# SyncE's first loads in a four-block transformer kernel: x of batches 2 and 3 wait for W_k, W_o moves behind the middle parts of batch 0

## Chip, cores and metric

One core of a Trainium2 chip runs the whole kernel in one launch. The metric is the device time in microseconds (us), the median of several executions; smaller is better.

## What is computed

Four residual blocks, each followed by a layer norm, over x of 4 batches x 256 tokens x 256 features in fp32: causal attention with 16 heads of 16, a gated feed-forward block of width 704, a second attention with biases, and a second feed-forward block of width 1024 with ternary weights.

```
x = layernorm(x + attention0(x, w_project, w_out))
x = layernorm(x + ffn0(x, gate_w, up_w, down_w, gate_s, up_s, down_s))
x = layernorm(x + attention1(x, Wq, bq, Wk, bk, Wv, bv, Wo, bo))
x = layernorm(x + ffn1(x, ternary(W_up), ternary(W_gate), ternary(W_down)))

attention: q, k, v = projections of x
           softmax(causal(q @ k.T / 4)) @ v, then @ w_out.T
```

## The kernel before

Each batch goes through every block on its own. The order of the work of each of the five engines is written out by hand, as a text of steps `STEP:lbi`, where l is the layer, b the batch and i the part (`QK:000` is the q projection of layer 0, batch 0, `QK:001` its k projection, `QK:000-1` both). An engine walks its list in order and waits on semaphores; nothing overtakes on one engine.

Precision comes from splitting. A weight or an activation is kept as a high part and the rest (`wa_hi` and `wa_lo`, `xT_hi` and `xT_lo`), and a product takes three matmuls (lines 566 to 568). q and k are cut into three bf16 parts, high (`QK`), middle (`MID` on SyncE, `SPLIT` on the computing engines) and low (`LO`). SyncE stacks the parts into `q_stack` and `k_stack` with a DMA for each place that a part has in the stack: three for a high part, two for a middle one, one for a low one, each 128 KB. TensorE's first score product `S:000` waits for all twelve of batch 0.

The beginning is what the change touches:

- SyncE (line 481 on) issues the four quarters of layer 0's attention weights, each 256 KB (`load_a0(sp, n)`, line 472: W_q, W_k, W_v, W_o for n = 0 to 3) and x of batches 1 to 3 (`load_x`, line 476), then the list `SYNC_STEPS`: `LOAD:003` is W_o, `LOAD:001` three small loads of biases (lines 520 to 522), then the stacks (line 538).
- ScalarE loads the transposed x of batch 0 itself (line 789). Step `PREPA` n (line 795) copies quarter n into `wa_hi` and waits for that quarter's load; its list reads `... SPLIT:010 PREPA:002 SPLIT:011 PREPA:003 QK:020-1 SPLIT:020-1 QK:030 ...`.
- VectorE takes the rest of each quarter (`PREPA`, line 966) and the rest of q and k (`QK`, line 994): `... QK:011 QK:020 PREPA:002 QK:021 PREPA:003 S:000-2 QK:030 S:003-7 ...`. `S` (line 1009) takes the maxima of a score tile out of PSUM and sets its banks free for TensorE, `MB` (line 1032) joins them, `MX` (line 1041) makes the low part of the maxima, which SyncE sends into the stack (line 545) ahead of the second score product `ST`.
- TensorE: `QK:000 XI:010 QK:001 QK:010 XI:020 XI:030 QK:011 QK:020-1 QK:030 S:000-2 V:000 S:003-7 ...`. `XI` (line 592) transposes x of a batch and waits for its load.

```
if step == "PREPA":
    c = slice(i * D, (i + 1) * D)
    act.wait_ge(a0_in[i], 16)
    nc.scalar.activation(wa_hi[:, :, c], raw_a[:, :, c], ACT.Copy).then_inc(wa0_hi, 1)
```

W_o itself is first multiplied in step `O:000`, some 40 us later; the space `raw` in which the quarters land is taken again by the load `RAW:000`, which waits for all four `PREPA` of VectorE.

Of the kernel before, what the change touches and what calls it, by code (L numbers as in the profile page):

```python
# [147 lines left out]
    HI:120 LN:310 HI:121-3 HI:130-3 LN:320 LT:130-1  # L148
"""
SYNC_STEPS = """  # L150
    LOAD:003 LOAD:001 QK:000-1 MID:000-1 LO:000-1 QK:010-1 LO:010-1 MID:010-1 RAW:000 LOAD:000 LO:020 RAW:001 LO:021
    MX:000 ML:000 MID:020-1 QK:020-1 RAW:002 MX:010 RAW:003 QK:030-1 ML:010 RAW:004-5 MID:030 LO:030-1 MID:031
    LOAD:002 RAW:006 MX:020 ML:020 RAW:007-10 MX:030 ML:030 RAW:0011-25 QK:100 RAW:0026-27 MID:100-1 RAW:0028 QK:101
    LO:100-1 RAW:0029-30 QK:110 MID:110-1 QK:111 LO:110-1 QK:120 MX:100 ML:100 LO:120-1 QK:121 MID:120-1 MX:110
# [26 lines left out]
def program(nc, x_nat, x_tr, a0, f0gu, f0dn, gs, us, ds_row, a1, bqk, bv, bo_row, f1, out):  # L181
# [13 lines left out]
    def nth(step, l=0, b=0, i=0):  # L195
        return count[(step, l, b, i)]
# [12 lines left out]
    def nb_of(l, b):  # L209

        return NB * l + b

    def users(l, b):

        return batches[max(0, nb_of(l, b) - SLOTS):max(0, nb_of(l, b) - SLOTS + 1)]
# [14 lines left out]
    with ctx:  # L230
# [3 lines left out]
        def sem(name):  # L234
            return ctx.enter_context(nc.semaphore(name))
# [73 lines left out]
        a0_in = [sem(f"a0_in{n}") for n in range(4)]  # L309
# [131 lines left out]
        def raw_of(piece, width):  # L441

            r = PIECES.index(piece)
            first = 1024 * (r % 2) if r < PREP0 else 512 * ((r - PREP0) % 2)
            return raw[:, first:first + width]
# [6 lines left out]
        def raw_used(piece):  # L452

            kind, n = piece
            return {"PREP0": (w_lo, n + 1) if n < 4 else (dn_scaled, n - 3), "PREP1": (w_lo, PREP0 + n + 1),
                    "AB": (abs_done, n + 1), "TERN": (tern_done, n + 1)}[kind]
# [6 lines left out]
        def columns_of(n):  # L463

            m, r = n // 4, n % 4
            r = (0, 2, 1, 3)[r] if m < 2 else r
            return m, slice(512 * r, 512 * (r + 1))

        def load_a0(queue, n):

            c = slice(n * D, (n + 1) * D)
            queue.dma_start(raw_a[:, :, c], a0[:, :, c]).then_inc(a0_in[n], 16)

        def load_x(queue, b):

            queue.dma_start(x[:, TT * b:TT * (b + 1), :], x_nat[:, TT * b:TT * (b + 1), :]).then_inc(x_in[b], 16)
# [4 lines left out]
        @block.sync  # L481
        def _(sp):

            load_a0(sp, 0)
            load_a0(sp, 1)
            load_x(sp, 1)
            load_a0(sp, 2)
            load_x(sp, 2)
            load_x(sp, 3)

            for step, l, b, i in sp_order:

                if step == "RAW":
                    kind, n = PIECES[i]
                    if i < 2:
                        sp.wait_ge(wa0_lo, 4)
                    elif i < PREP0 or i >= PREP0 + 2:
                        sp.wait_ge(*raw_used(PIECES[i - 2]))
                    else:

                        sp.wait_ge(*raw_used(PIECES[PREP0 - 1]))
                    landed = raw_in[i % 2]
                    if kind == "PREP0" and n < 4:
                        sp.dma_start(raw_of(PIECES[i], W0), f0gu[:, n // 2, (n % 2) * W0:(n % 2 + 1) * W0]).then_inc(landed, 16)
                    elif kind == "PREP0":
                        sp.dma_start(raw_of(PIECES[i], 512), f0dn[:, (n - 4) * 512:(n - 3) * 512]).then_inc(landed, 16)
                    elif kind == "PREP1":
                        sp.dma_start(raw_of(PIECES[i], 512).rearrange("p (k n) -> p k n", k=KT),
                                     a1[:, :, n * D:(n + 1) * D]).then_inc(landed, 16)
                    else:  # L510
                        m, c = columns_of(n)
                        sp.dma_start(raw_of(PIECES[i], 512), f1[:, m, c]).then_inc(landed, 16)
                if step == "LOAD":

                    if i == 0:
                        sp.dma_start(gs_c[:, :], gs).then_inc(scales_in, 16)
                        sp.dma_start(us_c[:, :], us).then_inc(scales_in, 16)
                        sp.dma_start(ds_b[:, :], ds_row.partition_broadcast(P)).then_inc(scales_in, 16)
                    if i == 1:
                        sp.dma_start(qk_bias[:, :], bqk).then_inc(bias_in, 16)  # L520
                        sp.dma_start(bv_c[:, :], bv).then_inc(bias_in, 16)
                        sp.dma_start(bo_b[:, :], bo_row.partition_broadcast(P)).then_inc(bias_in, 16)
                    if i == 2:
                        load_x(sp, 0)
                    if i == 3:
                        load_a0(sp, 3)
                if step in ("QK", "MID", "LO"):
                    n = nb_of(l, b) % SLOTS
                    stack, stacked, blocks = ((q_stack[n], q_stacked[n], Q_BLOCKS),
                                              (k_stack[n], k_stacked[n], K_BLOCKS))[i]  # L530
                    part, done = {"QK": (0, qk_hi), "MID": (1, qk_mid), "LO": (2, qk_lo)}[step]
                    if users(l, b):

                        sp.wait_ge(st_mm, nth("ST", *users(l, b)[0], NS - 1))
                    sp.wait_ge(done, nth("QK", l, b, i))
                    for r in range(len(blocks)):
                        if blocks[r] == part:
                            sp.dma_start(stack[r:KP:len(blocks), :, :].rearrange("p h t -> p (h t)"),
                                         part_of[nb_of(l, b) % 2][i][part][:, :]).then_inc(stacked[part], 16)
                if step in ("MX", "ML"):  # L540

                    n = nth("MX", l, b, i)
                    row, done, part = (KP, maxT_hi_done, maxT_hi) if step == "MX" else (KP + 1, maxT_done, maxT_lo)
                    sp.wait_ge(done, n)
                    sp.dma_start(q_stack[nb_of(l, b) % SLOTS][row:row + 1, HH * i:HH * (i + 1), :].rearrange("p h t -> p (h t)"),
                                 part[n % 2][:, :]).then_inc(max_rows[n % 2], 16)
                if step == "LN" and l == 3:
                    sp.wait_ge(ln_done, nth("LN", l, b))
                    sp.dma_start(out[:, TT * b:TT * (b + 1), :], x[:, TT * b:TT * (b + 1), :]).then_inc(stored, 16)
                if step == "LT":  # L550
                    sp.wait_ge(tail_done, i + 1)
                    sp.dma_start(out[:, TT * b + i:TT * b + i + 1, :], x[:, TT * b + i:TT * b + i + 1, :]).then_inc(stored, 16)
            sp.wait_ge(stored, 16 * (NB - 1 + TT))
# [234 lines left out]
        def _(act):  # L788
            act.dma_start(xT_raw[:, :, :], x_tr).then_inc(xT_in, 16)
            for step, l, b, i in act_order:  # L790
# [57 lines left out]
                if step == "ST":  # L848
                    n = nth("ST", l, b, i)
                    if n == 1:  # L850
                        act.wait_ge(xT_done, NB)
                    act.wait_ge(st_mm, n)
                    if n > 4:

                        _, pl, pb, ps = st_steps[n - 5]
                        act.wait_ge(pv_mm, nth("PV", pl, pb, ps // 2))
                    nc.scalar.activation(probs[(n - 1) % 4][:, :, :], place(key)[:, :, 0:T + P], ACT.Exp,  # L857
                                         scale=SC).then_inc(exp_done, 1)
# [493 lines left out]
```

## Time and profile before

| | |
|---|---|
| median of 3 runs | 252.99 us (252.36 to 253.24) |
| the profiled execution, its own time | 253.66 us |
| its span, first to last instruction | 251.8 us |
| TensorE busy | 239.2 us, 95% of the span |
| VectorE, ScalarE, GpSimd busy | 197.1, 159.8, 169.5 us |
| mean granted TensorE clock | 0.995 |

The busy times add up to far more than the span, since the engines run beside one another. TensorE has 12.6 us in which it does nothing, and its matmuls are pipelined, so that busy is not the same as fast. The profiled execution is 0.67 us slower than the median of the runs.

### The profile page before, as it was taken

How to read it: one execution, taken by the hardware profiler on the slowest of the kernel's cores; microseconds unless marked ns; L12 is line 12 of the kernel's file. 1: busy time of each engine (PE TensorE's matmuls, PEld its weight loads, DVE VectorE, ACT ScalarE, POOL GpSimd, SP SyncE). 2: the span in 40 equal slices, each digit the busy share in tenths (PEclk: the TensorE clock that was granted, in tenths of full speed). 3: DMA queues.
4: the chain of work that ended last, by engine and by line, in shares of the span. 5: the costliest groups of instructions: out<-in, count | busy, mean ns of one | idle time of the engine just before them, and what ended most of it. 6: DMA issues, size and time to landing. Idle time of an engine off the chain costs nothing.

```text
span 251.8 us, 6727 instructions
## 1 busy us (share of the span) xinstructions
PE 239.2 (95%) x2398; PEld 216.6 (86%) x2398; DVE 197.1 (78%) x591; ACT 159.8 (63%) x290; POOL 169.5 (67%) x226
## 2 busy tenths in 40 slices
PE   8898999999999999999999999989989999999991
PEld 8797898878789889999999997676678998999980
DVE  2459995968967576997989999999998619866674
ACT  4583169297788979637654367847797963655451
POOL 8584031837876762979929349887877975965663
PEclk9999999999999999999999999999999999999997
DMA  5967767773132342244555024464001000010003
GB/s 152 261 172 201 182 183 210 214 178 127 51 122 84 97 156 88 83 129 146 166 172 144 3 64 118 141 187 132 4 4 45 0 4 0 3 42 1 3 0 125
DMA packets 23312, 26.39 MB, mean 105 GB/s; under 512 B 3184, under 2 KB 18288, under 8 KB 23280
## 3 DMA queue, kind: packets, MB, share of 16 engines
q1 hardware_dynamic: 23136, 25.71, 35.8%
q8 instruction: 19, 0.31, 0.5%
q10 hardware_dynamic: 144, 0.26, 0.4%
q14 instruction: 13, 0.11, 0.1%
HBM read 12.20 MB, written 1.05 MB: 53 GB/s over the span
## 4 chain that ended last, share of the span: by engine, by line
PE 73%; DVE 7%; DMA 7%; ACT 4%; issue 4%; SPq 2%; POOL 2%; POOLq 0%; ACTq 0%; DVEq 0%
PE psum L566 10%; PE psum L567 9%; PE psum L568 9%; PE psum L741 6%; PE psum L742 6%; PE psum L686 5%; PE psum L661 5%; DMA x<-x_nat 3%; PE psum L775 3%; PE psum L776 2%; PE psum L629 2%; PE psum L689 2%; PE psum L664 2%; PE psum L633 2%; DMA k_stack<-k_part 2%
## 5 line engine op out<-in xcount | busy, mean ns | idle before, releaser
L857 ACT ACTIVATE probs<-psum 128x768 f32<-128x768 f32 x64 | 48.8, 808 | 12.4 <-PE psum L664 10.3
L1264 POOL TENSOR_TENSOR hidden<-hf,hidden 128x512 fp32r<-128x512 f32 x24 | 31.3, 1310 | 16.1 <-ACT hidden L899 16.0
L1224 POOL TENSOR_SCALAR_AFFINE_SELECT probs<-probs 128x512 f32<-128x512 f32 x48 | 30.9, 654 | 11.0 <-ACT probs L857 10.3
L1009 DVE TENSOR_REDUCE block_max<-psum 128x6 f32<-128x768 f32 x32 | 28.6, 944 | 2.6 <-PE psum L633 2.5
L661 PE MATMUL psum<-q_stack,k_stack 98*128 98x256 bf16 x128 | 28.3, 275 | 1.8 <-ACT probs L857 1.4
L1109 DVE SCALAR_TENSOR_TENSOR hf<-th,psum 128x512 f32<-128x512 f32 x28 | 19.1, 681 | 12.1 <-ACT th L888 4.3
L1020 DVE CUSTOM_DVE_ANT_0 masked<-psum,mask 128x256 bf16<-128x256 f32 x64 | 26.5, 415 | 1.3 <-issue 0.7
L566 PE MATMUL psum<-xT_hi,gu_hi 128*128 128x256 f32 x88 | 25.5, 289 | 0.0
L567 PE MATMUL psum<-xT_lo,gu_hi 128*128 128x256 f32 x88 | 24.9, 283 | 0.0
L568 PE MATMUL psum<-xT_hi,gu_lo 128*128 128x256 f32 x88 | 24.9, 283 | 0.0
L664 PE MATMUL psum<-q_stack,k_stack 98*128 98x128 bf16 x128 | 24.6, 218 | 0.0
L899 ACT ACTIVATE hidden<-hf 128x512 fp32r<-128x512 f32 x28 | 17.4, 629 | 8.1 <-DVE hf L1119 2.9
L873 ACT ACTIVATE x<-res,offset,rstd 128x256 f32<-128x256 f32 x30 | 16.3, 592 | 8.7 <-POOL offset L1206 8.7
L686 PE MATMUL psum<-probs,v_aug 128*32 128x256 f32 x256 | 20.2, 386 | 0.0
L1287 POOL TENSOR_SCALAR below_of<-raw,of_matrix 128x512 bf16<-128x512 f32 x12 | 19.6, 1638 | 0.0
L1270 POOL TENSOR_TENSOR gu_lo<-raw,gu_hi 128x704 fp32r<-128x704 f32 x4 | 6.7, 1680 | 19.2 <-ACT gu_hi L905 19.2
L566 PE MATMUL psum<-xT_hi,wa_hi 128*128 128x256 f32 x64 | 19.1, 298 | 0.1
L629 PE MATMUL psum<-k_stack,q_stack 96*128 96x256 bf16 x64 | 17.5, 273 | 1.6 <-DMA k_stack<-k_part 1.0
L567 PE MATMUL psum<-xT_lo,wa_hi 128*128 128x256 f32 x64 | 18.2, 284 | 0.0
L568 PE MATMUL psum<-xT_hi,wa_lo 128*128 128x256 f32 x64 | 18.2, 284 | 0.0
L1023 DVE CUSTOM_DVE_ANT_0 masked<-psum,mask 128x128 bf16<-128x128 f32 x64 | 18.2, 284 | 0.0
L661 PEld LDWEIGHTS psum<-q_stack,k_stack 98*128 98x128 bf16 x128 | 12.4, 97 | 6.5 <-ACT probs L857 1.7
(168 smaller groups left out, 897.6 us busy)
## 6 DMA issues: line engine op xcount, KB each, us to landing
q_stack<-q_part SPq DMA_DIRECT2D x48, 128.0 KB, 2.8
k_stack<-k_part SPq DMA_DIRECT2D x48, 128.0 KB, 2.5
raw<-f SPq DMA_DIRECT2D x24, 256.0 KB, 2.8
raw<-a SPq DMA_DIRECT2D x8, 256.0 KB, 4.1
raw<-f0gu SPq DMA_DIRECT2D x4, 352.0 KB, 4.5
x<-x_nat SPq DMA_DIRECT2D x4, 256.0 KB, 6.6
raw<-f0dn SPq DMA_DIRECT2D x3, 256.0 KB, 3.8
out<-x SPq DMA_DIRECT2D x3, 256.0 KB, 2.3
```

What stands on the lines that cost most here:

```text
L566: nc.tensor.matmul(o, w_hi, m_hi, start=first, stop=False, skip_group_check=shared)
L567: nc.tensor.matmul(o, w_hi, m_lo, start=False, stop=False, skip_group_check=shared)
L568: return nc.tensor.matmul(o, w_lo, m_hi, start=False, stop=last, skip_group_check=shared)
L629: nc.tensor.matmul(o[:, P:3 * P], q[0:KP, h, P:T], k[0:KP, h, :], start=True, stop=False, skip_group_check=True)
L661: nc.tensor.matmul(first_keys(o[:, j, 0:T + P]), k[r, h, 0:P], q[r, h, :].rearrange("p (c t) -> p c t", t=P), start=True, stop=not shut, s ...
L664: last = nc.tensor.matmul(o[:, j, P:T], k[r, h, P:T], q[r, h, P:T], start=False, stop=not shut, skip_group_check=True)
L686: last = nc.tensor.matmul(oo.rearrange("p (c t) -> p c t", t=P), v, first_keys(pr[:, j, :]), start=True, stop=False)
L857: nc.scalar.activation(probs[(n - 1) % 4][:, :, :], place(key)[:, :, 0:T + P], ACT.Exp, scale=SC).then_inc(exp_done, 1)
L1009: nc.vector.tensor_reduce(block_max[b % 2][:, 2 * i:2 * i + 2, 1:4], both(key)[:, :, 0:3 * P].rearrange("p j (c t) -> p j c t", t=P), mybi ...
L1020: nc.vector.tensor_tensor_reduce(out=masked[:, j, 0:T], in0=o[:, 0:T], in1=mask[:, 0:T], scale=1.0, scalar=NEG, op0=ALU.add, op1=ALU.max, ...
L1224: pool.affine_select(out=diag, in_=diag, compare_op=ALU.is_ge, fill=0.0, base=0, pattern=[[0, 2], [0, 2], [1, P]], channel_multiplier=-1). ...
L1264: pool.tensor_tensor(hidden[(n - 1) % NHID][1][:, :, :], hf[n % 2][:, :].rearrange("p (a t) -> p a t", a=2), hidden[(n - 1) % NHID][0][:, ...
```

## The change

SyncE waits for W_k (`a0_in[1]`) between the load of W_v and the loads of x for batches 2 and 3. W_o (`LOAD:003`) no longer stands ahead of the biases and the stacks, but behind `MID:000-1`, the middle parts of batch 0's stacks, and ahead of the low parts. Nothing else differs; the lines below the insertion move by two.

```
--- before.py
+++ after.py
@@ -148,7 +148,7 @@
 SYNC_STEPS = """
-    LOAD:003 LOAD:001 QK:000-1 MID:000-1 LO:000-1 QK:010-1 LO:010-1 MID:010-1 RAW:000 LOAD:000 LO:020 RAW:001 LO:021
+    LOAD:001 QK:000-1 MID:000-1 LOAD:003 LO:000-1 QK:010-1 LO:010-1 MID:010-1 RAW:000 LOAD:000 LO:020 RAW:001 LO:021
@@ -485,6 +485,8 @@
             load_a0(sp, 1)
             load_x(sp, 1)
             load_a0(sp, 2)
+
+            sp.wait_ge(a0_in[1], 16)
             load_x(sp, 2)
             load_x(sp, 3)
```

SyncE's order before, from the second instruction of the loads to the first low part of batch 0 (`a0` are the weights of layer 0's attention):

```order
L476 DMA x<-x_nat 128x512
L472 DMA raw<-a0 128x2x256
L476 DMA x<-x_nat 128x512 x2
L472 DMA raw<-a0 128x2x256
L520 DMA qk_bias<-bqk 128x4
L521 DMA bv_c<-bv 128x2
L522 DMA bo_b<-bo 128x256
L538 DMA q_stack0<-q_part0_0 16x8x512 [waits qk_hi]
...
L538 DMA k_stack0<-k_part1_0 16x8x512
L538 DMA q_stack0<-q_part2_0 16x8x512 [waits qk_lo]
```

And after the change, the same stretch:

```order
L476 DMA x<-x_nat 128x512
L472 DMA raw<-a0 128x2x256
L476 DMA x<-x_nat 128x512 [waits a0_in1]
L476 DMA x<-x_nat 128x512
L522 DMA qk_bias<-bqk 128x4
L523 DMA bv_c<-bv 128x2
L524 DMA bo_b<-bo 128x256
L540 DMA q_stack0<-q_part0_0 16x8x512 [waits qk_hi]
...
L540 DMA k_stack0<-k_part1_0 16x8x512
L472 DMA raw<-a0 128x2x256
L540 DMA q_stack0<-q_part2_0 16x8x512 [waits qk_lo]
```

The last load of a quarter went past three bias loads and ten stack DMAs; the two loads of x carry a wait.

ScalarE's order around its use of that quarter, after the change (it is the same as before, but for the line numbers, which were two lower):

```order
L815 ACTIVATE k_part0_1<-psum 128x512 [waits qk_mm]
L834 ACTIVATE q_part1_1<-q_left 128x512 [waits qk_left]
L797 ACTIVATE wa_hi<-raw 128x2x256 [waits a0_in2]
L834 ACTIVATE k_part1_1<-k_left 128x512 [waits qk_left]
L797 ACTIVATE wa_hi<-raw 128x2x256 [waits a0_in3]
L815 ACTIVATE q_part0_0<-psum 128x512 [waits qk_mm,q_stacked0_0]
L815 ACTIVATE k_part0_0<-psum 128x512 [waits qk_mm,k_stacked0_0]
L834 ACTIVATE q_part1_0<-q_left 128x512 [waits qk_left,q_stacked0_1]
```

Nothing moved here: the copy of W_o still stands between batch 1's middle part of k and the projections of batch 2.

## Rows read from the trace of the kernel before

**Rows 1.** The page: busy time of each engine.

```profile
PE 239.2 (95%) x2398; PEld 216.6 (86%) x2398; DVE 197.1 (78%) x591; ACT 159.8 (63%) x290; POOL 169.5 (67%) x226
```

**Rows 2.** Busy us by stretch, granted clock, DMA share and GB/s.

```profile
0.00:20.00 20.00, 17.39 (x118) 16.64 (x118) 8.49 (x14) 12.02 (x20) 14.82 (x32) 1.00 0.71 194
20.00:55.00 35.00, 34.53 (x396) 29.85 (x396) 30.95 (x49) 19.15 (x31) 12.40 (x9) 1.00 0.73 197
```

**Rows 3.** The chain that ended last, at the start: start us, us, what.

```profile
2.19 6.51 DMA x<-x_nat
...
17.68 2.40 DMA k_stack<-k_part
```

**Rows 4.** SyncE's timeline: start us, us, engine line op out<-in xcount.

```profile
5.13 1.37 SPq L520 DMA_DIRECT2D qk_bias<-bqk  x1
...
8.50 2.02 SPq L538 DMA_DIRECT2D q_stack<-q_part  x3
11.49 1.84 SPq L538 DMA_DIRECT2D k_stack<-k_part  x3
...
14.66 1.25 SPq L538 DMA_DIRECT2D k_stack<-k_part  x2
15.96 1.68 SPq L538 DMA_DIRECT2D q_stack<-q_part  x1
...
26.69 0.46 SPq L516 DMA_DIRECT2D gs_c<-gs  x1
...
32.39 0.59 SPq L545 DMA_DIRECT2D q_stack<-maxT_lo  x1
```

**Rows 5.** Single DMA issues in order (batch 0's x, W_k, batch 2's x, maxima): us to landing.

```profile
probs<-x_tr ACTq DMA_DIRECT2D x1, 256.0 KB, 2.8
...
raw<-a SPq DMA_DIRECT2D x1, 256.0 KB, 5.6
...
x<-x_nat SPq DMA_DIRECT2D x1, 256.0 KB, 6.6
...
q_stack<-maxT_lo SPq DMA_DIRECT2D x1, 8.0 KB, 2.6
```

**Rows 6.** ScalarE's timeline, copies of W_k and W_o, with [idle before <-releaser].

```profile
7.19 0.63 ACT L795 ACTIVATE wa_hi<-raw 128x512 fp32r<-128x512 f32 x1 [2.28 <-DMA raw<-a]
...
16.97 0.62 ACT L795 ACTIVATE wa_hi<-raw 128x512 fp32r<-128x512 f32 x1
```

**Rows 7.** VectorE's timeline.

```profile
18.71 0.68 DVE L966 TENSOR_TENSOR wa_lo<-raw,wa_hi 128x512 fp32r<-128x512 f32 x1
...
19.91 1.45 DVE L966 TENSOR_TENSOR wa_lo<-raw,wa_hi 128x512 fp32r<-128x512 f32 x1
21.29 2.68 DVE L1009 TENSOR_REDUCE block_max<-psum 128x6 f32<-128x768 f32 x3
...
29.84 0.21 DVE L1032 TENSOR_REDUCE row_max<-block_max 128x32 f32<-128x64 f32 x1
...
31.77 0.41 DVE L1041 TENSOR_TENSOR maxT_lo<-psum,maxT_hi 16x256 bf16<-16x256 f32 x1 [0.25 <-ACT maxT_hi L847]
```

**Rows 8.** TensorE's timeline: x's transposes, first score product, maxima, second score product.

```profile
8.75 0.66 PE L592 MATMUL psum<-ident,x 128*128 128x128 f32 x4 [0.91 <-DMA x<-x_nat]
...
12.42 1.03 PE L592 MATMUL psum<-ident,x 128*128 128x128 f32 x8
...
20.43 0.27 PE L629 MATMUL psum<-k_stack,q_stack 96*128 96x256 bf16 x1 [1.01 <-DMA k_stack<-k_part]
...
30.69 0.38 PE L649 MATMUL psum<-ident,row_max 128*128 128x128 f32 x2
...
35.14 0.27 PE L661 MATMUL psum<-q_stack,k_stack 98*128 98x256 bf16 x1
```

**Rows 9.** DMA queues from 15.8 to 17.3 us; the page's row on weight loads.

```profile
q8 instruction: 1, 0.02, 5.7%
...
raw<-a SPq DMA_DIRECT2D x8, 256.0 KB, 4.1
```

More of the change, by code:

```diff
@@ L150 @@
 SYNC_STEPS = """
-    LOAD:003 LOAD:001 QK:000-1 MID:000-1 LO:000-1 QK:010-1 LO:010-1 MID:010-1 RAW:000 LOAD:000 LO:020 RAW:001 LO:021
+    LOAD:001 QK:000-1 MID:000-1 LOAD:003 LO:000-1 QK:010-1 LO:010-1 MID:010-1 RAW:000 LOAD:000 LO:020 RAW:001 LO:021
     MX:000 ML:000 MID:020-1 QK:020-1 RAW:002 MX:010 RAW:003 QK:030-1 ML:010 RAW:004-5 MID:030 LO:030-1 MID:031
@@ L487, in _ @@
             load_a0(sp, 2)
+            sp.wait_ge(a0_in[1], 16)
             load_x(sp, 2)
```

## The prediction

> **What bounds the kernel now.** I read the page first: TensorE is busy for 239.2 of 251.8 us [rows 1], so a delay pays in full once it has reached TensorE, and a gain is worth only what TensorE idles. Then the stretches: in the first 20 us TensorE is busy for 17.39, in the next 35 us for 34.53 [rows 2]. The beginning is a chain of latencies, and behind it lies a long run without a gap in which an early delay could sink. Then the chain that ended last: it goes through x of batch 1, issued at 2.19 and landing 6.51 later, at 8.70, and later through the low part of k, whose DMA is issued at 17.68 and lands 2.40 later [rows 3]; `S:000` starts at 20.43 [rows 8]. Last the timelines. SyncE issues stacks almost without a pause from 11.49 on [rows 4]. ScalarE copies W_o at 16.97, without a wait [rows 6]. VectorE's low part of W_o ends directly before its first maxima at 21.29 [rows 7], 0.86 after `S:000` started. So two paths meet in the first maxima: the stacks through SyncE, and W_o's copy with batch 2's projections through ScalarE and VectorE.
>
> **The hold on x.** SyncE stands still behind W_v until W_k has landed. W_k took 5.6 from its issue [rows 5] and ScalarE, idle for it, starts at 7.19 [rows 6]. So x of batch 2 is issued at 7.2, x of batch 3 at 7.85 (a stack DMA and the gap behind it take 0.65 [rows 4]). TensorE transposes both from 12.42 on [rows 8]. A 256 KB load with nothing ahead of it took 2.8, x of batch 2 behind five others 6.6 [rows 5]. Now only the rest of two loads and x of batch 2 are ahead; I take 3.2, near the lower end, and x of batch 3 lands at 11.0. The cover is 1.4 us, the cost nothing. With 6.6 it would be 14.4, and TensorE would lose 2.0.
>
> Queued behind the waiting SyncE are biases and stacks. The first bias issue took 1.37 against 0.46 for its like at 26.69 [rows 4]; I put the difference on the loads then outstanding. Now fewer are, and three biases at 0.5 each run from 8.4 to 9.9. The high part of q, issued at 8.50 before, takes 2.0 for its three DMAs, and the high part of k starts at 11.9 instead of 11.49 [rows 4]: +0.4 on SyncE. If the first bias stays as slow as it was, +1.3.
>
> **W_o's move.** The issue leaves a place in which SyncE now stands still anyhow, and adds 0.65 between middle and low parts. The low parts are 0.4 + 0.65 = 1.05 late, so `S:000` would start at 21.5. Its six matmuls of 0.11 must end before the first maximum, which started 0.86 after `S:000`: a slack of some 0.3, so that this path alone costs +0.7.
>
> The larger effect is on ScalarE. The middle part of k ends at 15.91 [rows 4], now at 16.3, and W_o is issued. The issue at 15.96 took 1.68 where the others take 0.6 [rows 4], and in that stretch one instruction load of 16 KB stands on the DMA rings [rows 9]. It comes with an engine's progress and not with SyncE's place in its list, so I let it hit W_o's issue, which becomes effective at 17.05. 256 KB on quiet rings takes 2.8 [rows 5]; with stacks beside it I take 3.05. **W_o lands at 20.1**, and ScalarE, which copied it at 16.97, stands still for 3.1 us. From below: an issue at 16.3 without that pause and 2.8 give 19.1, a stand of 2.1. From above: the slow bias (+0.9) and the median of all weight loads in `raw`, 4.1 [rows 9], give 22.05, a stand of 5.1. I stay near the lower end, since the rings at 16 us carry little besides the stacks.
>
> Behind the copy on ScalarE stand batch 2's projections; VectorE stands in order behind the first of them, then takes W_o's low part, and only then the maxima. The way from 16.97 on ScalarE to 21.29 on VectorE is work or waits on each other [rows 6, 7], so the maxima start 3.1 late, at 24.4. By then the stacks (21.5) are no longer the later path, and their +0.7 is hidden. From there VectorE takes one maximum after another, three in 2.68, until the join at 29.84, which ends at 30.05 [rows 7] and now at 33.15. VectorE's next pause, 0.25 ahead of the low part of the maxima at 31.77 [rows 7], shrinks: 3.1 - 0.25 = 2.85. That part's DMA is issued at 32.39 and lands 2.6 later, at 34.99 [rows 4, 5], and the second score product begins 0.15 behind it, at 35.14 [rows 8]. It is 2.85 - 0.15 = **2.7 us late**. The transposes of the maxima, at 30.69 [rows 8], had 0.64 and are 2.5 late, which asks for no more. After that TensorE's work has no gap up to 55 us that could take this back [rows 2], and the later steps of the other engines wait for TensorE, or for loads that SyncE issues on their signals, so they are as late.
>
> One term could vanish: VectorE's low part of W_o took 1.45 at 19.91 where its twin took 0.68 [rows 7]. Its surroundings hang on ScalarE's same steps and move along, so I keep it; without it the sum is 0.77 smaller.
>
> **Sum.** 0 (hold) + 2.7 (W_o) + 0 (stacks, hidden) = +2.7. The profiled execution's own time of 253.66 becomes 256.4. It lay 0.67 above the median of 252.99, so against the runs the forecast is **255.7**. This case's own range: below, a stand of 2.1 less 0.4 of slack less 0.77, +0.9, 253.9; above, 5.1 less 0.4, +4.7, 257.7, cut to 257.6.
>
> Row and rule. W_k is there at 7.19 and x of batch 1, issued next, at 8.70 [rows 3, 6]: they land in the order of their issue, and the sum gives the hold nothing. The Trainium skill, page "DMA: Bandwidth & Descriptors", section "Queues, rings and completion order", has each DMA engine consume the descriptors of one issuing queue in ring order. By that rule, too, the held loads never stood ahead of W_k or of x of batch 1, and the hold gains nothing.
>
> **Rival 1: the early loads get faster.** W_k took 5.6 and x of batch 1 6.51 where 256 KB took 2.8 at the start [rows 3, 5]. If the outstanding loads slowed them, the hold gives back up to the 0.91 that TensorE idled before 8.75 [rows 8]. Then SyncE's stacks are 0.9 earlier, W_o is issued at 15.4 and lands at 18.2: a stand of 1.2 instead of 3.1, less 0.4 of slack: +0.8, and with VectorE's 0.77 gone, 0. Time 253.0 to 253.8, hardly to be told from no change. Against it stands the order of landing. Chance 13%. The same page, in "Latency and other measured facts", puts HBM's latency at 0.2 us on average and 2 us at high load, which would favour this case; no row here shows the latency alone.
>
> **Rival 2: faster.** The same gain of 0.91 at 8.75, with W_o in time. It decides at the moment when ScalarE is ready for the copy, 16.97 - 0.9 = 16.1: W_o must have landed by then, or 0.4 later. An issue at 15.4 with the shortest load, 2.8, lands at 18.2, 1.7 too late, so SyncE's ten stack DMAs would have to be issued faster than in 0.65 each. Price -0.9: 252.1. Chance 6%.
>
> **Rival 3: only the stacks count.** If W_o lands by 17.6 after all, the stacks' +0.7 is left: 253.7. It lies within rival 1's interval and shares its chance. That the hold does nothing at all is the sum's first term.
>
> **Rival 4: worse.** Slow biases and a slow W_o together, or x of batch 3 past 12.42: above 257.6, at +5 258.0. Chance 6%.
>
> **The numbers.** 75% for 253.9 to 257.6 with 255.7 likeliest, 13% for rival 1, 6% faster, 6% above. About 0.3%, 0.76 us, is what a measurement of this kernel can tell from no change. The range of 8 in 10 is 253.5 to 257.6: the main case and the upper half of rival 1. Faster 0.06, same 0.14, slower 0.80.
>
> **What would show it.** Right: ScalarE's copy (line 797) at about 20.1, after 3 us of idle released by the DMA raw<-a; VectorE's first maxima at about 24.4; TensorE's transposes of the maxima at 33.2 and second score product at 37.8; everything later shifted alike; the transposes of batches 2 and 3 still at 12.4. Wrong: W_k well before 7.19, TensorE's first transposes before 8.7, W_o's copy within 1 us of 16.97, or a shift at 35 us that has shrunk by 60.

## The result and the profile after

| | before | after |
|---|---|---|
| time, median (lowest to highest) | 252.98 us (252.36 to 253.48), 6 runs | 255.94 us (255.38 to 257.12), 6 runs |
| ratio, 95% interval | 1 | 1.0111 (1.0082 to 1.014) |
| profiled execution: own time, span | 253.66, 251.8 | 256.6, 254.7 |
| mean granted clock of TensorE | 0.995 | 0.983 |

The change makes the kernel slower by 2.96 us, or 1.1%, where +2.7 and 255.7 had been forecast. Both profiled executions lie 0.7 us above their medians, so their traces can be laid side by side.

The page and the stretches of the changed kernel (for [rows 1] and [rows 2]; the two short stretches also as they were before, in the second fence):

```profile
PE 242.0 (95%) x2398; PEld 219.0 (86%) x2398; DVE 196.2 (77%) x591; ACT 159.5 (63%) x290; POOL 169.9 (67%) x226
0.00:20.00 20.00, 17.54 (x118) 16.89 (x118) 6.58 (x10) 9.62 (x16) 14.51 (x31) 1.00 0.63 188
20.00:55.00 35.00, 33.55 (x342) 29.38 (x343) 29.77 (x46) 17.86 (x29) 11.54 (x8) 0.90 0.67 185
20.00:25.00 5.00, 3.56 (x20) 2.90 (x21) 3.50 (x5) 3.34 (x6) 1.90 (x2) 0.59 0.74 205
25.00:30.00 5.00, 5.00 (x40) 4.56 (x39) 4.69 (x6) 0.60 (x1) 0.78 (x1) 0.73 0.75 206
```

```profile
20.00:25.00 5.00, 4.57 (x46) 4.27 (x47) 5.00 (x6) 1.82 (x3) 2.34 (x2) 1.00 0.75 204
25.00:30.00 5.00, 4.96 (x47) 4.41 (x46) 4.92 (x8) 0.60 (x1) 0.00 (x0) 1.00 0.75 197
```

The first 20 us are as full as before. The loss is in the next ten: TensorE gets through 20 and 40 matmuls where it had done 46 and 47, and here the granted clock, 1.00 before (2.4 GHz), is 0.59 and 0.73 on average: for much of the time it was at the lower level, 1.2 GHz. TensorE's busy time of the whole rises by 2.8 us with the same 2398 matmuls: they took longer.

SyncE's timeline after (for [rows 4]):

```profile
7.06 0.82 SPq L476 DMA_DIRECT2D x<-x_nat  x2
7.92 0.43 SPq L522 DMA_DIRECT2D qk_bias<-bqk  x1
8.39 0.43 SPq L523 DMA_DIRECT2D bv_c<-bv  x1
8.87 0.43 SPq L524 DMA_DIRECT2D bo_b<-bo  x1
9.35 1.95 SPq L540 DMA_DIRECT2D q_stack<-q_part  x3
11.34 1.93 SPq L540 DMA_DIRECT2D k_stack<-k_part  x3
13.31 1.25 SPq L540 DMA_DIRECT2D q_stack<-q_part  x2
14.61 2.21 SPq L540 DMA_DIRECT2D k_stack<-k_part  x2
16.86 0.60 SPq L472 DMA_DIRECT2D raw<-a  x1
17.50 0.62 SPq L540 DMA_DIRECT2D q_stack<-q_part  x1
18.17 0.60 SPq L540 DMA_DIRECT2D k_stack<-k_part  x1
...
35.99 0.59 SPq L547 DMA_DIRECT2D q_stack<-maxT_lo  x1
```

The hold ends at 7.06, the biases are issued in 0.43 each, and the high part of k, at 11.34, is not later than the 11.49 of before. One issue is long: the middle part of k takes 2.21 for two DMAs that take 1.25 elsewhere. It is the pause of [rows 4] at 15.96, now 0.7 us earlier and in another DMA. W_o is issued at 16.86.

ScalarE (copies of W_k and W_o, for [rows 6]), then VectorE (for [rows 7]):

```profile
7.06 0.63 ACT L797 ACTIVATE wa_hi<-raw 128x512 fp32r<-128x512 f32 x1 [2.17 <-DMA raw<-a]
...
20.35 0.63 ACT L797 ACTIVATE wa_hi<-raw 128x512 fp32r<-128x512 f32 x1 [4.12 <-DMA raw<-a]
```

```profile
23.31 1.45 DVE L968 TENSOR_TENSOR wa_lo<-raw,wa_hi 128x512 fp32r<-128x512 f32 x1
24.68 2.67 DVE L1011 TENSOR_REDUCE block_max<-psum 128x6 f32<-128x768 f32 x3
...
28.26 5.28 DVE L1011 TENSOR_REDUCE block_max<-psum 128x6 f32<-128x768 f32 x6 [0.31 <-PE psum L635]
33.46 0.21 DVE L1034 TENSOR_REDUCE row_max<-block_max 128x32 f32<-128x64 f32 x1
...
35.37 0.41 DVE L1043 TENSOR_TENSOR maxT_lo<-psum,maxT_hi 16x256 bf16<-16x256 f32 x1 [0.24 <-ACT maxT_hi L849]
```

ScalarE, which had copied W_o at 16.97 without a wait, stands for 4.12 us and copies it at 20.35. The first maxima start 3.39 late and the join 3.62 late. TensorE (for [rows 8]):

```profile
7.92 0.60 PE L594 MATMUL psum<-ident,x 128*128 128x128 f32 x4
...
11.58 1.04 PE L594 MATMUL psum<-ident,x 128*128 128x128 f32 x8
...
21.45 0.37 PE L631 MATMUL psum<-k_stack,q_stack 96*128 96x256 bf16 x1 [2.72 <-DMA k_stack<-k_part]
...
21.93 0.42 PE L631 MATMUL psum<-k_stack,q_stack 96*128 96x256 bf16 x1
22.14 0.31 PE L633 MATMUL psum<-k_stack,q_stack 96*128 96x128 bf16 x1
...
34.29 0.38 PE L651 MATMUL psum<-ident,row_max 128*128 128x128 f32 x2
...
38.63 0.27 PE L635 MATMUL psum<-above,ident_b 128*128 128x256 bf16 x1
38.74 0.27 PE L663 MATMUL psum<-q_stack,k_stack 98*128 98x256 bf16 x1
```

And the chain that ended last, where it passes from the stacks to the first scores (for [rows 3]):

```profile
16.44 1.14 POOL k_part L1219
17.58 0.55 SPq L540
18.17 2.93 DMA k_stack<-k_part
```

TensorE stands for 2.72 us ahead of `S:000`, where it had stood for 1.01, and goes on at the lower clock: the same score matmul takes 0.37 instead of 0.27. The chain goes through this wait, not through ScalarE's. Behind 21.45 TensorE waits for nothing until 0.42 us ahead of batch 3's first scores, at 59.20. The second score product, too, stands directly behind the matmul before it; the low part of the maxima, issued at 35.99, had landed 1.9 later, at 37.9. So the forecast wait is there, but in this execution TensorE was not held by the late maxima. It was held by a wait that the forecast had called hidden, and by the lower clock behind it.

### The profile page after: what moved, and what is told of

Same layout as the page of the kernel before. It is cut to its first block, busy times and chain, and to the rows that moved or that the text cites. A ratio compares the mean times of both kernels' runs of the same rounds, so it can differ in the third digit from the quotient of the medians.

```text
span 254.7 us, 6727 instructions
## 1 busy us (share of the span) xinstructions
PE 242.0 (95%) x2398; PEld 219.0 (86%) x2398; DVE 196.2 (77%) x591; ACT 159.5 (63%) x290; POOL 169.9 (67%) x226
## 4 chain that ended last, share of the span: by engine, by line
PE 80%; DVE 6%; ACT 4%; issue 4%; DMA 2%; POOL 2%; SPq 2%; POOLq 0%; ACTq 0%; DVEq 0%
PE psum L568 10%; PE psum L570 10%; PE psum L569 10%; PE psum L743 6%; PE psum L744 6%; PE psum L688 6%; PE psum L663 5%; PE psum L631 3%; PE psum L635 3%; PE psum L691 3%; PE psum L777 2%; PE psum L666 2%; PE psum L778 2%; DMA k_stack<-k_part 2%; PE psum L584 2%
## 5 line engine op out<-in xcount | busy, mean ns | idle before, releaser
L631 PE MATMUL psum<-k_stack,q_stack 96*128 96x256 bf16 x64 | 18.5, 289 | 3.1 <-DMA k_stack<-k_part 2.7
L635 PE MATMUL psum<-above,ident_b 128*128 128x256 bf16 x64 | 18.5, 288 | 0.0
## 6 DMA issues: line engine op xcount, KB each, us to landing
raw<-f SPq DMA_DIRECT2D x24, 256.0 KB, 2.8
raw<-a SPq DMA_DIRECT2D x8, 256.0 KB, 3.8
x<-x_nat SPq DMA_DIRECT2D x4, 256.0 KB, 3.6
raw<-f0dn SPq DMA_DIRECT2D x3, 256.0 KB, 2.9
out<-x SPq DMA_DIRECT2D x3, 256.0 KB, 2.3
```

The lines of the kernel that those rows point to most:

```text
L631: nc.tensor.matmul(o[:, P:3 * P], q[0:KP, h, P:T], k[0:KP, h, :], start=True, stop=False, skip_group_check=True)
```

## The experiments

Ratios are to the kernel before on the same chip, measured together. The times of one kernel spread more in these measurements than in the first measurement (the kernel before from 251.6 to 256.6 us), so the intervals are some 0.25 to 0.45% to either side. A profiled execution can lie 1 us from its kernel's median.

**The parts alone.** Only the hold:

```diff
             load_a0(sp, 2)
+            sp.wait_ge(a0_in[1], 16)
             load_x(sp, 2)
```

> Only the hold on x of batches 2 and 3; W_o stays ahead of the biases. Theory A (W_o's late landing is the whole loss, the hold costs nothing): x of batch 1 lands at 7.7 as in the changed kernel instead of 8.7, ScalarE copies W_o without a wait at about 16.3, the first maxima on VectorE come at 21.3 or up to 0.7 earlier, and the time is 252.3 to 253.0 us. Theory B (the hold is part of the loss, since TensorE then ends its projections 0.7 us earlier and idles 1.7 instead of 1.0 us ahead of the first scores, and its granted clock falls as in the changed kernel, 0.59 from 20 to 25 us): clock below 0.9 in 20 to 25 us, time 253.5 to 255.

Only W_o's move:

```diff
-    LOAD:003 LOAD:001 QK:000-1 MID:000-1 LO:000-1
+    LOAD:001 QK:000-1 MID:000-1 LOAD:003 LO:000-1
```

> Only the move of W_o behind the middle parts; no hold. Theory A: W_o lands at 20 to 20.5 us, ScalarE stands 3.1 to 3.5 us, first maxima at 24.5 to 24.8, time 255.5 to 256.2. Theory B (in the changed kernel half of the loss needs the fallen clock, for which TensorE must idle 2.7 us ahead of the first scores): here TensorE is 0.7 us later at its projections and idles about 1.9 us, so if the clock stays at 1.00 the shift at 35 us is 2.7 to 3.1 instead of 3.6 and the time 255.2 to 255.7; if it falls all the same, as A.

Measured: the hold alone 254.81 against 253.60, ratio 1.004 (1.0008 to 1.0072); the move alone 255.90, ratio 1.0094 (1.0057 to 1.0132). The hold alone, on TensorE, ScalarE and VectorE:

```profile
20.57 0.37 PE L630 MATMUL psum<-k_stack,q_stack 96*128 96x256 bf16 x1 [2.12 <-DMA k_stack<-k_part]
```

```profile
15.91 0.62 ACT L796 ACTIVATE wa_hi<-raw 128x512 fp32r<-128x512 f32 x1
```

```profile
21.93 3.06 DVE L1010 TENSOR_REDUCE block_max<-psum 128x6 f32<-128x768 f32 x3 [2.39 <-PE psum L634]
```

W_o is in time there and nobody waits for it, yet the maxima are 0.64 late and wait for TensorE, whose clock is 0.66 from 20 to 25 us, as Theory B has it. The move alone:

```profile
19.50 0.63 ACT L795 ACTIVATE wa_hi<-raw 128x512 fp32r<-128x512 f32 x1 [3.99 <-DMA raw<-a]
```

```profile
20.59 0.27 PE L629 MATMUL psum<-k_stack,q_stack 96*128 96x256 bf16 x1 [2.48 <-DMA k_stack<-k_part]
```

Here both waits are there without the hold, and the clock fell all the same, so that the time is Theory A's; TensorE's gap of 2.48 had been expected at 1.9. So W_o's move carries most of the loss, and the hold, forecast at 0, costs something too: some 1.0 us, with 0.2 to 1.8 as its interval. The two together (1.34%) are more than the change has (1.11%), by less than the intervals.

**Take TensorE's idle time away.** Products of ones, ahead of `S:000`, into the PSUM bank that the first scores then overwrite, in the changed kernel. They add work and leave none out:

```diff
+                        if nb_of(l, b) == 0:
+                            spare = take(key, 0)
+                            for _ in range(11):
+                                nc.tensor.matmul(spare[:, 0:P], ones[:, :], ones[:, :], start=True, stop=True)
```

> The changed kernel with eleven 128x128 products of ones on TensorE in the gap of 2.7 us ahead of the first scores, written to the bank that the first scores then overwrite; they take about 2.5 us at the full clock. The copy of W_o still stands in its place. Theory A (ScalarE's stand of 3.4 us sets the end, the clock adds the rest): granted clock 1.00 in 20 to 30 us, maxima still at 24.7, the join of the maxima at 33.1 instead of 33.46, shift at 35 us 3.1 to 3.3 instead of 3.6, time 255.3 to 255.7. Theory B (the fallen clock is the whole loss): the shift is 1 us or less, time 253.0 to 254.0.

Measured: 258.14, ratio 1.0176 (1.0144 to 1.0209), above both expectations and slower still. The clock is 1.00 in all stretches and the gap ahead of the scores 0.31, but W_o is copied at 19.99 and the maxima start at 24.33: ScalarE's path alone holds them. The join, at 32.71, is earlier than in the change, but batch 3's first scores are later (59.81 against 59.20), and so is the end. The trace has 22 more of TensorE's records, and an instruction load stands at 42.6 us where the change has one at 44.5. SyncE's issue beside it, a weight load at 42.43, takes 1.52 us where its like at 44.58 takes 0.58:

```profile
42.43 1.52 SPq L506 DMA_DIRECT2D raw<-f0gu  x1
43.99 0.54 SPq L547 DMA_DIRECT2D q_stack<-maxT_hi  x1
44.58 0.58 SPq L506 DMA_DIRECT2D raw<-f0gu  x1
```

That such shifted loads make the kernel slower is not shown; but it is no clean test, and I made the fill again with few wide products, and joined as many of the warm-up's, so that the number of TensorE's instructions stays (`of_ones(o, n)` is one product of ones, n times 128 columns wide):

```diff
-            for _ in range(WARM):
-                nc.tensor.matmul(psum[:, 7, 0:P], ones[:, :], ones[:, :], start=True, stop=True)
+            for r in range(WARM - 3):
+                of_ones(psum[:, 7, :], 2 if r < 3 else 1)
...
+                        if nb_of(l, b) == 0:
+                            spare = take(key, 0)
+                            for _ in range(3):
+                                of_ones(spare, 4)
```

> The changed kernel with its gap ahead of the first scores filled by three products of ones with 512 columns, and three of the eleven products at the start joined into wider ones, so that TensorE's program has as many instructions as before from the first scores on (in e3_fill 22 more pushed its instruction loads to other places, and its shift grew from 2.8 us at 38 us to 3.8 at 54 us and 4.3 at 174 us). Theory A' (ScalarE's stand for W_o alone costs 2.7 to 3.0 us; e3's extra is the moved instruction loads): clock 1.00 in 20 to 30 us, shift 2.7 to 3.0 at 38 us and the same at 200 us, ratio to before 1.009 to 1.012. Theory C (a filled TensorE costs by itself): shift grows behind 38 us as in e3, ratio 1.016 or more.

Measured: 256.57 against 253.23, ratio 1.013 (1.0091 to 1.0169). The clock is 1.00 and the join, 33.46 in the change, starts at 31.97; ScalarE still stands for W_o:

```profile
19.25 0.63 ACT L805 ACTIVATE wa_hi<-raw 128x512 fp32r<-128x512 f32 x1 [3.56 <-DMA raw<-a]
```

Here the late maxima do hold TensorE, which waits twice for VectorE to set banks free, 0.48 and 0.23 us. The first of these waits:

```profile
24.59 0.28 PE L639 MATMUL psum<-k_stack,q_stack 96*128 96x256 bf16 x1 [0.48 <-DVE block_max L1019]
```

The ratio is just above Theory A' (1.009 to 1.012), and its interval reaches into Theory C (1.016 or more), and overlaps with that of the eleven products. So the clock is kept, ScalarE's stand is left, and the kernel is no faster than the change.

**Take ScalarE's stand away.** The changed kernel with the copy of W_o later on ScalarE and VectorE:

```diff
-    PREPA:002 SPLIT:011 PREPA:003 QK:020-1 SPLIT:020-1 QK:030
+    PREPA:002 SPLIT:011 QK:020-1 SPLIT:020-1 PREPA:003 QK:030
...
-    QK:011 QK:020 PREPA:002 QK:021 PREPA:003 S:000-2 QK:030
+    QK:011 QK:020 PREPA:002 QK:021 S:000-2 PREPA:003 QK:030
```

> The changed kernel with W_o's copy on ScalarE moved behind batch 2's middle parts, and W_o's low part on VectorE moved behind the first three maxima, so that nobody waits for W_o ahead of the first scores. Theory A: ScalarE does not stand, the maxima start at 22.3 (0.9 after the first scores at 21.45), the shift at 35 us is about 1, time 253.3 to 254.2. Theory B (a second, equal loss lies beside it: TensorE at half its clock from 21.45 to 27.4 delivers the fourth score tile at 28.2 whatever ScalarE does, where the maxima needed it at 24.5): clock 0.59 in 20 to 25 us, maxima idle for TensorE behind the third tile, shift at 35 us 3 us or more, time 255.2 to 256.

Measured: 256.14, ratio 1.0111 (1.0072 to 1.0149), the ratio of the change itself. Yet nobody stands for W_o ahead of batch 2's projections, which are copied from 15.75 on; what is left of the stand, 0.78, comes behind them:

```profile
20.09 0.63 ACT L797 ACTIVATE wa_hi<-raw 128x512 fp32r<-128x512 f32 x1 [0.78 <-DMA raw<-a]
```

```profile
22.05 2.69 DVE L1011 TENSOR_REDUCE block_max<-psum 128x6 f32<-128x768 f32 x3 [3.61 <-PE psum L635]
26.67 5.28 DVE L1011 TENSOR_REDUCE block_max<-psum 128x6 f32<-128x768 f32 x6 [0.74 <-PE psum L635]
31.87 0.21 DVE L1034 TENSOR_REDUCE row_max<-block_max 128x32 f32<-128x64 f32 x1
```

The maxima now wait for TensorE at both places, 3.61 and 0.74, and the join is 2.03 later than before the change, where the change has 3.62. But this difference is not what ScalarE's stand costs. TensorE waits for nothing between `S:000` and batch 3's first scores in either trace. The rest of the difference is in the clock, which fell later here and came back earlier:

```profile
20.00:25.00 5.00, 3.80 (x27) 3.62 (x28) 2.95 (x4) 1.23 (x2) 2.27 (x2) 0.76 0.73 203
25.00:30.00 5.00, 5.00 (x46) 4.55 (x45) 4.26 (x6) 0.60 (x1) 0.00 (x0) 0.90 0.70 193
```

From 20 to 30 us it is 0.83 on average against 0.66 in the change, which by an estimate (0.17 of 10 us) is worth up to 1.7 us, and `S:000` starts 0.25 earlier. Why the lower level lasts longer in the change is open.

**Take both away**, the two edits in one kernel:

> As e5, and W_o's copy and low part moved behind batch 2's projections as in e4_copy_later. Two parallel losses (ScalarE's stand; TensorE's gap of 2.75 us with the half clock behind it): with both out of the way only the stacks' lateness is left, first scores at 21.2 to 21.5, maxima at 22.1, shift 0.7 to 1.2 us at 38 us, ratio 1.002 to 1.005. If one of the two is not a cause: ratio 1.008 or more.

Measured: 255.64, ratio 1.0102 (1.0057 to 1.0147). That is above the expected 1.002 to 1.005, and by the expectation's own rule (1.008 or more) it speaks against one of the two as a cause of the time. In the trace ScalarE's stand and TensorE's gap are gone, and the join is only 0.85 late:

```profile
30.69 0.20 DVE L1042 TENSOR_REDUCE row_max<-block_max 128x32 f32<-128x64 f32 x1
```

But of 2.8 us won back at the join, 1.2 are left in the span (253.5 against 254.7). TensorE's next wait, ahead of batch 3's first scores, has become longer, 1.29 us where the change had 0.42:

```profile
57.79 0.27 PE L639 MATMUL psum<-k_stack,q_stack 96*128 96x256 bf16 x1 [1.29 <-DMA k_stack<-k_part]
```

**Fills where W_o is early.** The hold alone with two wide products, and the kernel before with one (the edit above with 2 and 1 in the place of 3):

> The kernel before with the hold on x alone, as e1_hold_only, and its gap of 2.1 us filled by two wide products with an unchanged instruction count. Theory: what the hold costs (e1: ratio 1.004, clock 0.66 in 20 to 25 us) is the half clock only: clock 1.00, first scores at 20.5, shift at 38 us 0 to 0.3 instead of 1.4, ratio 0.998 to 1.001. If the hold costs by another way (x of batches 2 and 3 late, SyncE behind): ratio 1.004 again.

> The kernel before with its gap of 1.0 us filled by one wide product, instruction count unchanged. If in part of its runs the gap is longer and the clock falls (its runs on this chip spread from 251.8 to 256.6): median 0.5 to 1 us lower and a smaller spread, ratio 0.995 to 0.998. If the gap of 1.0 us never costs clock: ratio 0.999 to 1.001.

Measured: 254.56, ratio 1.0051 (1.0025 to 1.0077), and 253.38, ratio 1.0006 (0.9973 to 1.0039). The clock is 1.00 in both. The second says that one wide product by itself costs and gives nothing that the interval shows. The first misses its main expectation (0.998 to 1.001) and falls to the other one, that the hold costs by another way than the clock. It joins at 30.22, 1.0 earlier than the hold alone, and its time is no lower than that kernel's.

**W_o one step earlier**, behind the high parts, with the hold:

```diff
-    LOAD:001 QK:000-1 MID:000-1 LOAD:003 LO:000-1
+    LOAD:001 QK:000-1 LOAD:003 MID:000-1 LO:000-1
```

> The change with W_o's issue one step earlier: behind the four high parts of batch 0, ahead of the middle parts; the hold stays. If it is W_o's landing after the place of its copy that costs beside the hold, W_o is issued at about 13.0 us here, behind k's high part, and lands at about 16.5: ScalarE's stand ahead of QK:020 (3 us and more in the change) shrinks to below 0.7, the first maxima start at 21.9 to 22.6 as in the run with the hold alone, and the time is that run's, 254.0 to 255.0. The rival, that the hold is the whole of the loss and W_o's place none, gives the same time as the hold alone too, but then also no difference from the change itself: 255.5 to 256.2. TensorE's gap ahead of S:000 stays at 2.0 to 2.7 us in either case, and the granted clock falls behind it.

Measured: 255.15 against 253.47, ratio 1.0069 (1.004 to 1.0098), between the hold alone and the change, and not to be told from either by time alone. The time lies between the two expectations, too (to 255.0, and from 255.5 on). In the trace W_o is issued at 12.47, and ScalarE and TensorE read:

```profile
16.66 0.63 ACT L797 ACTIVATE wa_hi<-raw 128x512 fp32r<-128x512 f32 x1 [1.18 <-DMA raw<-a]
```

```profile
20.39 0.27 PE L631 MATMUL psum<-k_stack,q_stack 96*128 96x256 bf16 x1 [2.49 <-DMA k_stack<-k_part]
```

The stand is 1.18 instead of 4.12 (0.7 had been expected), and no longer ends after the stacks: the maxima, at 21.24, wait for TensorE. Its gap stays at 2.49.

**Can the kernel before be beaten?** The later copy in the kernel before, without and with one wide product:

> No part of the change: the kernel before, with the copy of W_o (PREPA:003) put later on ScalarE (behind SPLIT:020-1) and its lower part later on VectorE (behind S:000-2). ScalarE has work ahead of QK:020 that is not wanted until V:000; if that work is on the path to the first maxima, they start 0.3 to 0.6 us earlier and the time falls by that to 252.4 to 252.9. The rival: the first scores wait for the stacks, whose DMAs SyncE issues in their own time, so a free ScalarE gives nothing, and the time is 252.8 to 253.6.

> The kernel before with both: the copy of W_o later, and one wide product of ones ahead of S:000 that keeps TensorE's gap there under 0.5 us with its instruction count unchanged. Each alone moved the trace's middle by 0.5 us or less. If the two losses that the change has are parallel ones that before hardly has, nothing is left to take: 252.6 to 253.4. If before still has 0.5 us of each, 252.0 to 252.5, faster than before by 0.2 to 0.4 %.

Measured: 254.10, ratio 1.0025 (1.0 to 1.005), and 254.23, ratio 1.0053 (1.0022 to 1.0084). Neither beats it, and both lie above all that was expected of them. The second's profiled execution joins 1.0 us earlier than the kernel before (28.84) and has a shorter span (251.4), but it was the fastest of its 12 runs, 0.9 below their median. No version run here is faster than the kernel before.

These kernels are also the right base for the change with the same edits. The change costs 1.0111 without any, 1.0111 / 1.0025 = 1.0086 with the later copy, and 1.0102 / 1.0053 = 1.0049 with both edits (one wide product in the one, three in the other). The last has an interval of some 0.55% to either side, and its distance from 1.0111 is 0.6%, just as much as the two intervals together allow. So it is possible that the two edits take away half of the change's cost and cost something themselves; it is not shown.

The landmarks of all traces, in us:

| kernel | gap ahead of `S:000`, its start | clock 20 to 25 | copy of W_o | first maxima | join | batch 3's first scores | span | ratio |
|---|---|---|---|---|---|---|---|---|
| before | 1.01, 20.43 | 1.00 | 16.97 | 21.29 | 29.84 | 55.76 | 251.8 | 1 |
| the change | 2.72, 21.45 | 0.59 | 20.35 | 24.68 | 33.46 | 59.20 | 254.7 | 1.0111 |
| hold only | 2.12, 20.57 | 0.66 | 15.91 | 21.93 | 31.22 | 58.05 | 254.0 | 1.004 |
| W_o only | 2.48, 20.59 | 0.66 | 19.50 | 23.84 | 32.22 | 58.17 | 253.7 | 1.0094 |
| change, 11 products | 0.31, 21.31 | 1.00 | 19.99 | 24.33 | 32.71 | 59.81 | 256.0 | 1.0176 |
| change, 3 wide | none, 20.73 | 1.00 | 19.25 | 23.59 | 31.97 | 58.71 | 254.5 | 1.013 |
| change, copy later | 2.75, 21.20 | 0.76 | 20.09 | 22.05 | 31.87 | 58.21 | 253.8 | 1.0111 |
| change, both | none, 20.85 | 1.00 | 19.69 | 21.70 | 30.69 | 57.79 | 253.5 | 1.0102 |
| hold, 2 wide | 0.95, 20.82 | 1.00 | 15.58 | 21.67 | 30.22 | 56.50 | 252.8 | 1.0051 |
| before, 1 wide | 0.37, 19.89 | 1.00 | 16.21 | 20.74 | 29.24 | 55.65 | 251.2 | 1.0006 |
| hold, W_o one step earlier | 2.49, 20.39 | 0.66 | 16.66 | 21.24 | 31.08 | 56.80 | 252.5 | 1.0069 |
| before, copy later | 1.22, 19.56 | 1.00 | 19.10 | 20.41 | 29.40 | 56.45 | 251.9 | 1.0025 |
| before, both | none, 19.00 | 1.00 | 18.93 | 19.85 | 28.84 | 55.30 | 251.4 | 1.0053 |

## Why the prediction was right, and where its steps were not

The time was right, 255.7 forecast and 255.94 measured. The forecast's mechanism, ScalarE's stand for W_o, is in the trace (the copy of W_o at 20.35, forecast at 20.1), and with the clock kept (change, 3 wide) it holds TensorE and the kernel is 1.3% slower. But in the profiled execution of the change it lay beside another loss of about the same length, and this other one held TensorE. That the sum came within 0.3 us is in part luck: the trace is 3.6 us late at the second score product, where 2.7 had been forecast, and 2.9 at the end.

**The hold on x costs 0: mis-sized.** Its cover was judged rightly: the transposes of batches 2 and 3 start at 11.58 and do not wait. SyncE was a little ahead of its forecast, with 9.35 for 9.9 and 11.34 for 11.9. The forecast put the 1.37 us of the first bias on the loads then outstanding; that did not hold for the most of it. Three kernels with the same loads ahead of it issue it in 0.60 to 0.70 (before with the later copy, with one wide product, with both). What the step left out is TensorE. The hold alone leaves `S:000` where it was (20.57 against 20.43), but TensorE is done with what stands ahead of it at 18.45 instead of 19.42, and idles 2.12 instead of 1.01, and behind this idle time its clock is 0.66. Alone, the hold measured +0.4%. That the clock is what makes it cost is not shown: with the gap filled and the clock at 1.00 it measured +0.5%.

**The early loads.** x of batch 1 took 5.6 us from its issue and not 6.5, and TensorE's transposes started at 7.92 instead of 8.75, without a wait behind the projection ahead of them. That had been named as a sign of rival 1. But it is not shown to come from the hold. The five traces without it have these transposes at 8.75, 7.20, 7.98, 7.66 and 7.51, the eight with it between 7.17 and 7.92. The profiled execution of before simply was the latest of all thirteen, so that all shifts against it are rather too small: before with one wide product, whose time is the same, joins at 29.24 and not at 29.84. If the hold gains anything here, it is less than this scatter.

**W_o's move.** ScalarE's copy was forecast at about 20.1, and came at 20.35. W_o took 3.5 from its issue at 16.86, where 3.05 from 17.05 had been forecast. The wait as such was forecast at 3.1 and is 4.12, because ScalarE came to it earlier. The instruction load hit SyncE at 15.2, within 0.8 of where it had been, as the forecast assumed ("with an engine's progress"); only it hit the middle part of k and not W_o's issue, which for W_o is the same delay. First maxima: 24.4 forecast, 24.68 measured. VectorE's 1.45 us for the low part of W_o stayed, as assumed.

**"By then the stacks are no longer the later path, and their +0.7 is hidden": the step that failed.** `S:000` came at 21.45, as forecast (21.5). But the score matmuls behind it did not take the 0.11 us each that the forecast counted. At the lower clock they take 0.21 (21.93 to 22.14 in the rows above). In the profiled execution this path is the one that TensorE follows without a further wait, and ScalarE's stand is what lies hidden beside it: even the maxima behind the first three wait for TensorE ([0.31 <-PE]). The join is 3.62 late. With the clock kept and ScalarE's stand left it is 2.13 late, with neither 0.85, close to the 0.7.

The clock does not set the time alone, though. It was recorded for all six executions of the change: 0.983, 0.983, 0.987, 0.991, 0.994 and 0.994 over the whole span, with 256.6, 256.09, 255.62, 255.38, 255.79 and 257.12 us. The last two clocks are those of kernels whose trace shows no fall (0.992 to 0.998 for the change with three wide products), and the times are no shorter. This fits two losses in parallel, each of which nearly covers the other; a trace of such an execution was not taken.

**From the join to the end.** The transposes of the maxima came at 34.29 (33.2 forecast), the second score product at 38.74 (37.8), 3.6 late instead of 2.7. The forecast had taken off 0.25 for VectorE's pause ahead of the low part of the maxima and 0.15 for the time behind its landing. The first is still there, with 0.24, and the second was no slack of this path, since TensorE came to the second score product without a wait in both traces. This 0.4 was taken off wrongly. Of the 3.6, 3.44 is left at batch 3's first scores and 2.9 at the end, so that what was won back behind it brought the span close to the forecast. That TensorE's work "has no gap up to 55 us that could take this back" held for the change. The wait just behind it, ahead of batch 3's first scores, is where some experiments lose a part of what they had won (the later copy, the three wide products, both): 0.42 in the change, 0.58 before, 1.01 to 1.72 in five of the others.

**The rivals.** Rival 1 has its first step in the trace and nothing of its price: W_o, issued at 16.86 and not at 15.4, was late. Rivals 2 and 3 are out, since W_o did not land by 17.6; yet rival 3's path, the stacks, is the one that held TensorE in the profiled execution, at far more than its +0.7. Rival 4's slow biases did not come.

**What stays open.** The traces show both losses up to 30 us. No time shows their removal: the change with neither loss is at 1.0102, the change at 1.0111, and the intervals leave some 0.5% either way between two such kernels. What the runs show beyond their intervals is that the change costs 1.1%, that the move alone costs 0.6% or more, and the hold alone something between 0.1 and 0.7%. Why the time of the kernel with both edits stays up is open. Its one trace has the longer wait at 57 us, and the kernel before is slower, too, with the same two edits.

## What to carry to other kernels

A load that is moved to a late place must be costed for the engine that stands in order at its use, and the same move for every DMA behind it in the issuing queue; here the two paths ran side by side and came out about equally late. Where a step makes TensorE wait longer, cost the matmuls behind the wait at the lower clock as well, and see in the trace which of the paths TensorE really waits for. Removing one of two parallel losses shows nothing in the time. Removing both did not show here either: follow the gain past the next wait before counting on it, and run the same edits in the kernel before, to see what they cost by themselves.

## What the runs showed of the hardware

- TensorE's clock fell behind single waits of 2.12 to 2.75 us, in every trace that has one (five of thirteen; from 20 to 25 us it is 0.59 to 0.76 on average), and stayed at 1.00 where the wait was 0.31 to 1.22. A score matmul of 256 columns stands 0.21 us from the next at the lower level and 0.11 at the higher. The Trainium skill, page "TensorE: Matmul & The Clock Gate", section "Back-to-back issue gap", gives the columns over 1.2 at the lower level, and over 2.4 with 2.5 ns added at the higher, which is 213 and 109 ns for 256; the trace agrees.
- A DMA that SyncE issues beside an instruction load (one packet of some 16 KB on the queue q8) takes 1.1 to 2.0 us instead of 0.6. The load comes at 14.8 to 16.6 us in all thirteen traces, whatever SyncE is issuing then: the low part of q in the kernel before, the middle part of k in the change, W_o itself in the change with both edits (1.55 us). That the load is what slows the issue, and that it is TensorE's, is inferred from their standing together.
- x of batch 1, issued at 2.17 to 2.19 us in all thirteen traces, took 4.7 to 6.5 us to land, with the same loads ahead of it; W_k was in use at 6.24 to 7.19.
